# Joined moving blocks in the 192 and 240 column bodies of a mixture-of-experts kernel, and another order of its splits

## The reference

```python
x = x + 0.5 * ffn(layernorm(x), gate_weight, wi, wo)
x = x + mixer(layernorm(x), Wu, bu, Wv, bv, Wg1, bg1, Wg2, bg2, conv_w, conv_b)
x = x + 0.5 * ffn(layernorm(x), gate_weight, wi, wo)

def ffn(inputs, gate_weight, wi, wo):      # 8 experts, hidden 512, inner 2048
    logits = tokens @ gate_weight.T
    top1 = argmax(logits)                  # one expert for each token
    # a token takes part if its rank in its expert is below C = 320
    hmid = gelu(dispatch @ wi)             # for each expert: tokens x 512 by 512 x 2048
    eout = hmid @ wo                       # tokens x 2048 by 2048 x 512
    # back to the tokens, times the softmax probability of the expert
```

## Time and profile before

| | us |
|---|---|
| median of 3 runs | 1094.91 |
| lowest, highest | 1094.69, 1099.75 |
| the profiled execution's own time | 1096.42 |
| its span in the profile | 1094.7 |
| TensorE matmul busy | 1044.4 |
| TensorE weight load busy | 987.2 |
| DVE, ACT, POOL busy | 721.1, 543.7, 144.3 |

### The profile page before, as it was taken

The page is one execution under the profiler, slowest core; times in us unless marked ns, Lnnn a source line. Parts: engine busy times, 40 slices in busy tenths (PEclk is TensorE's granted clock), DMA queues, the critical chain, the costliest instruction groups (busy, mean ns, idle before and its releaser), DMA issues.

```text
span 1094.7 us, 20908 instructions
## 1 busy us (share of the span) xinstructions
PE 1044.4 (95%) x7888; PEld 987.2 (90%) x7888; DVE 721.1 (66%) x1091; ACT 543.7 (50%) x851; POOL 144.3 (13%) x138
## 2 busy tenths in 40 slices
PE   9699999999999999599999996999999999999995
PEld 6699999999999999378777776999999999999995
DVE  8556565776577686477786774557777777665552
ACT  5445455565556565253342324355665656554441
POOL 3201111203021110100000022002212021130101
PEclk9899999999999999899999996999999999999998
DMA  8468546566464761500011244437566575664510
GB/s 309 176 240 303 185 173 215 181 222 206 161 235 156 251 208 38 178 1 1 1 39 39 80 144 147 153 116 244 202 229 213 190 244 185 228 211 142 169 39 25
DMA packets 83276, 177.32 MB, mean 162 GB/s; under 512 B 4192, under 2 KB 4704, under 8 KB 83168
## 3 DMA queue, kind: packets, MB, share of 16 engines
q1 hardware_dynamic: 75488, 152.61, 40.6%
q0 software_dynamic: 7168, 23.07, 6.0%
q10 hardware_dynamic: 576, 1.05, 0.3%
HBM read 162.04 MB, written 18.87 MB: 165 GB/s over the span
## 4 chain that ended last, share of the span: by engine, by line
PE 90%; DVE 4%; DMA 2%; issue 1%; ACT 1%; POOL 1%; POOLq 0%; ACTq 0%; SPq 0%; DVEq 0%
PE psH L1226 13%; PE psH L1227 13%; PE psH L1228 13%; PE acc L1234 12%; PE acc L1235 12%; PE acc L1233 12%; PE acc L1226 3%; PE acc L1228 3%; PE acc L1227 3%; DVE row_stats L831 1%; PE psH L1357 1%; PE psH L1458 1%; DVE dtl L798 1%; PE psT L1286 1%; PE psT L1559 1%
## 5 line engine op out<-in xcount | busy, mean ns | idle before, releaser
L1226 PE MATMUL psH<-dth,wih 128*128 128x240 f32 (+5 forms) x1024 | 295.0, 288 | 0.0
L1234 PE MATMUL acc<-htl,woh 128*128 128x240 f32 (+5 forms) x1024 | 293.4, 287 | 0.0
L1227 PE MATMUL psH<-dtl,wih 128*128 128x240 f32 (+5 forms) x1024 | 293.4, 287 | 0.0
L1235 PE MATMUL acc<-hth,wol 128*128 128x240 f32 (+5 forms) x1024 | 293.2, 286 | 0.0
L1228 PE MATMUL psH<-dth,wil 128*128 128x240 f32 (+5 forms) x1024 | 293.2, 286 | 0.0
L1233 PE MATMUL acc<-hth,woh 128*128 128x240 f32 (+5 forms) x1024 | 293.2, 286 | 0.0
L798 DVE TENSOR_TENSOR wol<-raw_wo,woh 128x1024 fp32r<-128x1024 f32 x128 | 155.7, 1223 | 146.6 <-ACT woh L615 143.5
L649 ACT ACTIVATE gel<-psH 128x320 f32<-128x320 f32 x256 | 111.8, 437 | 189.1 <-PE psH L1228 178.8
L615 ACT ACTIVATE woh<-raw_wo 128x1024 fp32r<-128x1024 f32 x128 | 134.6, 1059 | 132.3 <-PE acc L1235 132.1
L1226 PEld LDWEIGHTS psH<-dth,wih 128*128 128x128 f32 x1024 | 193.1, 189 | 0.4
L1227 PEld LDWEIGHTS psH<-dtl,wih 128*128 128x128 f32 x1024 | 193.0, 188 | 0.0
(11 more groups left out here) (195 smaller groups left out, 1145.4 us busy)
## 6 DMA issues: line engine op xcount, KB each, us to landing
raw_wi<-in_wi SPq DMA_DIRECT2D x64, 1024.0 KB
raw_wo<-in_wo SPq DMA_DIRECT2D x64, 1024.0 KB, 5.4
out_x<-xt SPq DMA_DIRECT2D x4, 1024.0 KB, 5.9
xt<-in_x SPq DMA_DIRECT2D x6, 512.0 KB, 8.2
xt<-x SPq DMA_DIRECT2D x3, 1024.0 KB, 9.7
raw_u<-in_wuT SPq DMA_DIRECT2D x1, 1024.0 KB
raw_u<-in_wvT SPq DMA_DIRECT2D x1, 1024.0 KB
xt<-in_x ACTq DMA_DIRECT2D x2, 256.0 KB, 3.8
```

The source lines that it names most:

```text
L1226: pe.matmul(out, lh, rh, start=first, stop=False)
L1227: pe.matmul(out, lh, rl, start=False, stop=False)
L1234: pe.matmul(out, lh, rl, start=False, stop=False, skip_group_check=True)
L1235: return pe.matmul(out, ll, rh, start=False, stop=False, skip_group_check=True)
```

## The change

1. `WIDTHS` becomes 192, 240, 272, 288, 304, 320. The body for 256 is gone; experts with up to 192 tokens have one of their own. "Narrow" is now up to 240. In the program's order 192 stands second, where 256 stood (`PLACED`), and the aligned addresses behind the first bodies keep the later ones in place.
2. The high and low part of the hidden values become one tile `ht`, [.., 2, CAP]. In bodies of up to 240 columns (`JOINT`) `onto` runs high weight x (high, low) as one matmul of 2 x w moving columns, whose results go to columns 0 to w and 256 to 256 + w of the bank. Then low weight x high follows as before.
3. DVE adds the second block to eoT after ACT's copy (L1092 in the changed kernel), 240 columns, four times an expert, in every expert. The factor `joint_now` is 1 for a joined expert and 0 for another. TensorE waits for this addition (`eoT_sum`) where it waited for the copy. The whole acc banks are set to zero at the start, and `clear_acc` multiplies by zeros (`nil`).
4. DVE's wo split for the next expert's step 0 moves from ahead of the tokens to behind the first row product, and in an expert's first pass the wo split of b moves behind the hidden split of a, and the hidden split of b ahead of the wi splits.

```diff
-WIDTHS = range(240, CAP + 1, 16)
+WIDTHS = (192, 240, 272, 288, 304, 320)
 NARROW = 2
-assert WIDTHS[NARROW - 1] <= 2 * P < WIDTHS[NARROW]
+JOINT = WIDTHS[NARROW - 1]
+PLACED = (240, 192, 272, 288, 304, 320)
+SECOND = 256
...
-        hth = put("hth", [P, 2, ICS, CAP], F32R)
-        htl = put("htl", [P, 2, ICS, CAP], F32R)
+        ht = put("ht", [P, 2, ICS, 2, CAP], F32R)
+        hth, htl = ht[:, :, :, 0, :], ht[:, :, :, 1, :]
...
-            pool.iota(least[:, :, :], [[0, E], [WIDTHS.step, NW - 1]], base=WIDTHS.start, channel_multiplier=0,
-                      allow_small_or_imprecise_dtypes=True).then_inc(pool_const, 1)
+            for k, w in enumerate(WIDTHS[:-1]):
+                ins = pool.memset(least[:, :, k:k + 1], float(w))
+            ins.then_inc(pool_const, 1)
...
+                then(dve.tensor_scalar(joint[:, :], ps_taken, JOINT + 0.5, None, ALU.is_lt))
...
             for bank in acc[:2]:
-                dve.memset(bank[:, 2 * P:CAP], 0.0).then_inc(banks_set, 1)
-            for bank in (*acc[2:], *psH):
+                dve.memset(bank[:, SECOND:], 0.0).then_inc(banks_set, 1)
+            for bank in acc[2:]:
+                dve.memset(bank[:, :], 0.0)
+            for bank in psH:
                 ins = dve.memset(bank[:, 0:CAP], 0.0)
...
+                    dve.tensor_copy(joint_now[:, 1 - a:2 - a], joint[:, bass.ds(e + 1, 1)])
...
                         a, b = 2 * i, 2 * i + 1
-                        wo_split(e, b)
+                        if i > 0:
+                            wo_split(e, b)
                         hidden_split(e, a)
+                        if i == 0:
+                            wo_split(e, b)
+                            hidden_split(e, b)
                         if not last or a + 2 < STEPS:
                             wi_split(e, a + 2)
-                        hidden_split(e, b)
+                        if i > 0:
+                            hidden_split(e, b)
...
-                        if not last or a + 2 < STEPS:
+                        if a + 2 < STEPS:
                             wo_split(e, a + 2)
 
+                    for c in range(DC):
+                        dve.wait_ge(s.acc_done, DC * (PAIRS * e + PAIRS) + c + 1)
+                        dve.wait_ge(s.eoT_copied, DC * e + c + 1)
+                        dve.scalar_tensor_tensor(eoT[:, c, 0:JOINT], acc[c][:, SECOND:SECOND + JOINT],
+                                                 joint_now[:, side:side + 1],
+                                                 eoT[:, c, 0:JOINT], ALU.mult, ALU.add).then_inc(s.eoT_sum, 1)
...
+                        if i == 0 and not last:
+                            wo_split(e + 1, 0)
...
+            def onto(bank, w, lhs, both):
+
+                lh, ll = lhs
+                if w <= JOINT:
+                    pe.matmul(bank.rearrange("p (r q) -> p r q", r=2)[:, :, 0:w], lh, both[:, :, 0:w],
+                              start=False, stop=False, skip_group_check=True)
+                else:
+                    for r in range(2):
+                        pe.matmul(bank[:, 0:w], lh, both[:, r, 0:w], start=False, stop=False, skip_group_check=True)
+                return pe.matmul(bank[:, 0:w], ll, both[:, 0, 0:w], start=False, stop=False, skip_group_check=True)
...
-                        pe.wait_ge(s.eoT_done, DC * e + c + 1)
+                        pe.wait_ge(s.eoT_sum, DC * e + c + 1)
```

More of the change, by code:

```diff
@@ L39 @@
 Q = E * CHUNKS
-WIDTHS = range(240, CAP + 1, 16)
+WIDTHS = (192, 240, 272, 288, 304, 320)
 NARROW = 2
-assert WIDTHS[NARROW - 1] <= 2 * P < WIDTHS[NARROW]
+JOINT = WIDTHS[NARROW - 1]
+PLACED = (240, 192, 272, 288, 304, 320)
+SECOND = 256
+assert JOINT <= SECOND and sorted(PLACED) == list(WIDTHS)
 GROUP = 4
@@ L1228, in product @@
                 return pe.matmul(out, ll, rh, start=False, stop=last)
-            def onto(out, lhs, rhs):
-                (lh, ll), (rh, rl) = lhs, rhs
-                pe.matmul(out, lh, rh, start=False, stop=False, skip_group_check=True)
-                pe.matmul(out, lh, rl, start=False, stop=False, skip_group_check=True)
-                return pe.matmul(out, ll, rh, start=False, stop=False, skip_group_check=True)
+            def onto(bank, w, lhs, both):
[7 more added lines that the diff above has]
+                return pe.matmul(bank[:, 0:w], ll, both[:, 0, 0:w], start=False, stop=False, skip_group_check=True)
             turned = []
@@ L1401, in _, with turn_tokens @@
                     peek()
-                def turn_tokens(e, c, chunks, s=s):
-                    for k in range(chunks):
-                        q = k * P
-                        ins = pe.transpose(TURNED[c][:, q:q + P], dn[:, k, c * P:(c + 1) * P], ident[:, :])
-                    ins.then_inc(s.tokT_done, 1)
+                def turn_tokens(e, chunks, s=s):
+                    pe.wait_ge(s.dn_done, CHUNKS * e + CHUNKS)
+                    for c in range(DC):
+                        if c < 2:
+                            pe.wait_ge(s.eoT_sum, DC * e + c + 1)
+                        for k in range(chunks):
+                            q = k * P
+                            ins = pe.transpose(TURNED[c][:, q:q + P], dn[:, k, c * P:(c + 1) * P], ident[:, :])
+                        ins.then_inc(s.tokT_done, 1)
                 def clear_acc():
                     for c in range(DC):
-                        pe.matmul(acc[c][:, 510:512], ones[:, :], ones[:, 0:2], start=True, stop=True)
+                        pe.matmul(acc[c][:, 510:512], ones[:, :], nil[:, :], start=True, stop=True)
                 def mm1(e, step, k, w, s=s):
@@ L1503, in _ @@
                         with nc.body(f"{what}_{n}", parent=head, valid_engines=[pe.engine]):
-                            pe.wait_ge(s.dn_done, CHUNKS * e + CHUNKS)
-                            for c in range(DC):
-                                if c < 2:
-                                    pe.wait_ge(s.eoT_done, DC * e + c + 1)
-                                turn_tokens(e, c, chunks)
+                            turn_tokens(e, chunks)
                             turn_out(e)
@@ L1515, in _ @@
                 over_bb = nc.cur_bb
-                for k, w in enumerate(WIDTHS):
+                for k, w in enumerate(PLACED):
                     with nc.body(f"run_{w}_{n}", parent=head, valid_engines=[pe.engine]):
```

20 lines of the change are left out of this document (13 added, 7 removed).

## The result

| | kernel before | changed kernel |
|---|---|---|
| median, us | 1097.18 (4 runs, 1094.69 to 1099.75) | 1084.96 (4 runs, 1083.39 to 1088.27) |
| ratio to before | | 0.9893, 95% interval 0.9868 to 0.9917 |
| a second comparison | 1095.03 (15 runs) | 1085.20 (5 runs), ratio 0.9905, 0.9889 to 0.9922 |
| profiled execution, its span | 1096.42, 1094.7 | 1083.39, 1081.6 |

What follows compares the result with a forecast made beforehand. TensorE (PE) was taken to bound the kernel, through distances between matmul starts. Terms -1.5 - 12.5 + 2.2 + 2.2 + 0.6 = -9.0 us, from a median of 1094.91 to 1085.9 us, range 1080 to 1092.

Steps and rivals of the forecast that it cites:

- The floor: On TensorE, about 112 ns per four-byte 128x128 weight load; a narrower matmul with its own load costs 112 whatever its width.
- Rival C: wi and wo weights load faster: all 384 matmuls at 192 columns come every 89.2 ns; time 1072.0 us; chance 6%.
- The law of the pair: A joined wo product costs the long matmul's streaming plus one 112 ns load: 287.2 ns at 192, 330.2 at 240.
- Rival E: Moving operands in two runs are dear: gain gone at 0.041 ns a column more, over 0.5% slower from 0.066; chance 8%.
- A joined matmul of over 0.19 us at 384 columns: Sign in the changed kernel's profile, in a 192 body, that would make the forecast wrong; 0.175 us was expected.
- rival B: The long product's weight loads during both matmuls, so a pair costs its streaming, 264.4 instead of 287.2 ns; 1081.7 us; 11%.
- Joined at 240: wo products in four 240 experts: two loads instead of three, 5.8 ns x 64 each, -1.5 us for four.
- 192 columns: Four second-layer experts go from 240 to 192: wo saves 48.8 ns x 64 each, -12.5 us; narrower wi matmuls 0.
- Does the shorter body starve PE: Whether the second hidden split is ready for a pass's second wo step: 2.2 us against 2.30 at 192, fits by 0.1.
- The additions: Vector engine's additions out of PSUM, 0.44 us each, make 14 expert entries 0.16 us late: +2.2 us (1.0 to 6.4).
- Rival D: An addition takes 0.74 us, an entry is 0.46 late, 14 cost 6.4 us; time 1090.7; chance 14%.
- The ends: At each layer's end the last transposes wait for the last addition, 0.32 us late: +0.6 us for two (0.5 to 1.2).

## Why the prediction was right, point by point

- **The floor.** That a weight load of 128x128 in four bytes takes 112 ns and that a matmul of less than 240 columns cannot come sooner had been read from one row of 96 columns. The run without joining shows it at 192 columns, 111.7 ns, the 176 body at 176 and the router's products at 8. Rival C is out: without joining, the kernel is 0.3% slower than before, not 1% faster or more.
- **The law of the pair.** Streaming of the long one plus one load: 287.2 forecast, 285 measured at 192 (medians); 330.2 and 327 at 240; 272.9 and 272 at 176. At 256 the short one's streaming, 120, is larger than the load, and 352.5 stands against 350. The line through 320 and 512 columns was thus right for two-run operands: the loads' starts have 176 and 218 ns for the 175.2 and 218.2 forecast. The estimate of 202.5 ns for 480 columns, from the formula of the Trainium skill that the prediction set beside it, was too low. The load's share is 108 rather than 112, which is why all sums are a little under the law's. Rival E, dear two-run operands, is out by the same numbers.
- **The signs were badly chosen.** "A joined matmul of over 0.19 us at 384 columns" was to make the forecast wrong, and L1266 at 0.09 was to speak for rival B. By the letter both came: the matmuls' recorded starts are 0.198 and 0.088 apart. A distance between two starts cannot tell the law from B, since B would shorten the whole period to 264 ns; measured are 285, and B is out.
- **Joined at 240** was sized at -1.5 us and measured -2.1: 64 pairs of 327 instead of 330 ns are 0.2 us less an expert.
- **192 columns** was sized at -12.5 and measured -11.6. Two things the sum did not have stand against each other. The wait in the fourth pass costs 0.2 to 0.3 us an expert; without it a 192 expert takes 39.65 us where no other wait falls in (the runs with the moved normalisation), 3.35 less than 43.00 where 3.12 had been sized, because pairs of 285 ns are 0.14 us and slightly faster wi matmuls 0.08 us less. "Does the shorter body starve PE" had been asked of the hidden splits alone, which fit by 0.1 us as computed (0.08 us of wait in some passes), and not of ScalarE's normalisations in the third pass.
- **256 to 272** +2.2, measured +2.1.
- **The additions.** 0.16 us an entry, measured 0.11, though one takes 467 ns rather than 440: the sum of hand-overs had been taken too long. 2.2 us in all became 1.5, and 1.6 by the run that leaves them out. Rival D is out. The ends were right, 0.3 us each.
- **The moved splits** were costed at nothing, with the cover named. The run with the old order shows that this was no ornament of the change: without it the additions would cost 3.2 us more. The prediction had not said so.
- **The program's place** was costed at nothing too. No entry of the changed kernel has such a wait, so that was right for the change as it stands, and only because it keeps six bodies and their order; two experiments that touch this lose 4.7 and 23 us, and the prediction had not seen how near that lay.
- The **total** was sized at -9.0. The medians moved by 12.2 and 9.8 us in the two comparisons (the ratios make it 11.7 and 10.4), the traces' own terms give -9.5. In the second comparison six of the 15 executions of the kernel before had a granted clock of 0.977 or less, and none of the changed kernel's five. Those above 0.977 have medians of 1094.46 and 1085.20 us, 9.3 apart. For the first comparison the clocks of the kernel before are not on record, and its surplus stays unassigned. So the mechanism and its sizes were right, while the time itself, 1084.96 for 1085.9, was in part luck: the forecast started from a median of 1094.91 where the comparison had 1097.18, and the executions of one kernel spread by 5 to 8 us.

## What to carry to other kernels

A stream of load and matmul pairs has two prices, the load and the streaming, and for each load with its matmul only the larger counts (here 112 ns against 0.448 ns a column): look for a row with few columns to read the load's price before you narrow anything, and below it join moving operands that share a weight. Take the sum of a change from pieces that both traces contain (experts, entries), not from the two spans, since one profiled execution can carry microseconds of another clock. And where the program jumps between bodies, count their blocks as a resource: one body too many cost here 23 us for the 2.7 that it gains in its own expert.

## What the runs showed of the hardware that was not expected

- In a pair of one long and one short matmul with a load each, the recorded starts of the matmuls divide the time as 0.20 and 0.09 us, those of their loads as 0.108 and 0.176. A single distance between recorded matmul starts is no price of one matmul; a whole period is, and the loads' starts show what it is made of.
- Float32 matmuls of 8 columns start 112 ns apart and bf16 ones of 8 columns 25 ns apart, each with a 128x128 load of its own.
- The granted clock at the second router was half for 20.5 us in three traces (two of the kernel before, one of a changed one) and for 10 to 14 us in the nine others of kernels with six widths, which do much the same work there. The stretch between the layers takes 233.6 to 235.0 us with the longer half-clock time and 230.5 to 232.7 with the shorter.
- With six bodies the queue that brings the program has two packets within the experts of layer one; with a seventh it has eight for the same five bodies run. Two entries then took 5.6 to 5.8 us instead of 3.1, and the second layer's first entry 12.5 us more than the tokens made it wait. With six bodies but another order of two of them one entry took 5.84. Which blocks give way was not worked out.
